# Expert layer of a small mixture-of-experts block: seven block products and one slot an expert

## What is computed

```python
h = ragged_dot(x_rep_sort, w1, group_sizes)                    # D = 1024 -> M = 3584, per expert
h = silu(h) * ragged_dot(x_rep_sort, w3, group_sizes)
out_sort = ragged_dot(h, w2, group_sizes)                      # M = 3584 -> D = 1024
out = einsum('tkd,tk->td', out_rep, topk_w)                    # two experts a token
x = x + out
```

## Time and profile before

| | us |
|---|---|
| Median of 3 runs (lowest, highest) | 8400.37 (8398.75, 8401.36) |
| The profiled execution, own time | 8408.29 |
| Its span, first to last instruction | 8406.7 |

### The profile page before, as it was taken

How to read it: one execution, slowest core, us unless ns; L and a number is a source line. 1 busy time by engine, 2 the same in 40 slices (tenths; PEclk the granted TensorE clock), 3 DMA queues, 4 the chain that set the end, 5 groups by cost and what they waited for, 6 DMA issues and landing times.

```text
span 8406.7 us, 119512 instructions
## 1 busy us (share of the span) xinstructions
PE 8220.8 (98%) x46092; PEld 7566.7 (90%) x46093; DVE 3531.5 (42%) x3602; ACT 3267.5 (39%) x3511; POOL 478.6 (6%) x580
## 2 busy tenths in 40 slices
PE   8959999999999999999999999999999999999998
PEld 5549999999999999999999999999999999999998
DVE  6755333443443334453333334453333334433343
ACT  2325333443333334453333334453333333433343
POOL 2320000000000000000000000000000000000000
PEclk8969999999999999999999999999999999999999
DMA  3335444553443434553434434554434344444343
GB/s 113 115 111 185 142 135 135 179 162 131 139 149 122 147 120 151 169 185 120 141 129 134 141 128 150 161 187 142 135 130 139 120 145 141 152 143 135 130 154 116
DMA packets 839095, 1189.77 MB, mean 142 GB/s; under 512 B 27872, under 2 KB 722400, under 8 KB 839072
## 3 DMA queue, kind: packets, MB, share of 16 engines
q1 hardware_dynamic: 812096, 1116.05, 40.5%
q0 software_dynamic: 26976, 73.42, 3.7%
HBM read 1121.90 MB, written 71.67 MB: 142 GB/s over the span
## 4 chain that ended last, share of the span: by engine, by line
PE 92%; ACT 0%; issue 0%; DVE 0%; DMA 0%; ACTq 0%; POOL 0%; POOLq 0%; DVEq 0%
PE p L1038 20%; PE p L1040 20%; PE p L1039 20%; PE acc L1063 10%; PE acc L1064 10%; PE acc L1062 10%; PE p L1093 1%; DVE lo L975 0%; ACT hi L921 0%; ACT L921 0%; DMA out_x<-y,id_s 0%; DMA xg<-x_rows,id_g 0%; DVE xlo L1001 0%; ACT xhi L946 0%; ACT y L963 0%
## 5 line engine op out<-in xcount | busy, mean ns | idle before, releaser
L1038 PE MATMUL p<-xhi,hi 128*128 128x384 f32 (+4 forms) x10752 | 3435.3, 320 | 30.6 <-DVE lo L975 19.1
L1040 PE MATMUL p<-xhi,lo 128*128 128x384 f32 (+4 forms) x10752 | 3432.7, 319 | 0.0
L1039 PE MATMUL p<-xlo,hi 128*128 128x384 f32 (+4 forms) x10752 | 3430.0, 319 | 0.0
L1038 PEld LDWEIGHTS p<-xhi,hi 128*128 128x128 f32 x10752 | 2029.1, 189 | 65.7 <-issue 41.3
L1039 PEld LDWEIGHTS p<-xlo,hi 128*128 128x128 f32 x10752 | 2030.5, 189 | 24.3
L1040 PEld LDWEIGHTS p<-xhi,lo 128*128 128x128 f32 x10752 | 2028.1, 189 | 0.0
L988 DVE TENSOR_TENSOR hid<-sil,p 128x384 f32<-128x384 f32 x672 | 372.4, 554 | 3764.0 <-PE p L1040 3764.0
L975 DVE TENSOR_TENSOR lo<-raw,hi 128x2048 fp32r<-128x2048 f32 x673 | 1543.4, 2293 | 792.8 <-ACT hi L921 792.8
L1062 PE MATMUL acc<-hi,hhi 128*128 128x512 f32 x3808 | 1497.6, 393 | 0.0
L1064 PE MATMUL acc<-hi,hlo 128*128 128x512 f32 x3808 | 1491.5, 392 | 0.0
L1063 PE MATMUL acc<-lo,hhi 128*128 128x512 f32 x3808 | 1490.6, 391 | 0.0
(11 more groups left out here) (181 smaller groups left out, 2439.4 us busy)
## 6 DMA issues: line engine op xcount, KB each, us to landing
raw<-in_L_ffn_w SPq DMA_DIRECT2D x1011, 1024.0 KB, 5.1
xin<-in_x SPq DMA_DIRECT2D x8, 2048.0 KB, 10.7
out_x<-x SPq DMA_DIRECT2D x32, 512.0 KB, 2.9
x_rows<-x SPq DMA_DIRECT2D x32, 512.0 KB, 3.7
ctxt<-in_ctx SPq DMA_DIRECT2D x4, 1024.0 KB, 9.6
table<-rec,posi POOLq DMA_INDIRECT x80
xg<-x_rows,id_g POOLq DMA_INDIRECT x75, 6.7
out_x<-y,id_s POOLq DMA_INDIRECT x72, 7.3
```

The lines of the kernel that those rows point to most:

```text
L1038: pe.matmul(bank[:, 0:n], hi13[par][:, a, k, :], xhi[:, k, 0:n], start=(k == 0), stop=False)
L1039: pe.matmul(bank[:, 0:n], hi13[par][:, a, k, :], xlo[:, k, 0:n], start=False, stop=False)
L1040: mm = pe.matmul(bank[:, 0:n], lo13[par][:, a, k, :], xhi[:, k, 0:n], start=False, stop=(k == KT - 1))
```

## The change

The attention part stays. In the expert stage the loops, the tiling and all buffers are new.

- **Slots.** A slot takes up to 1088 rows of one expert. Its rows are dealt to two halves (even and odd), and the width n of all matmuls is half the row count, rounded up to 8 and then to one of eight widths from 256 to 544. Above 512, a matmul is issued as two of n/2 columns into two PSUM banks. ScalarE and VectorE know three widths: 512, 528 and 544.
- **First product by seven block products.** A unit is one of w1, w3 with 256 hidden values. The weights (two halves of hidden values by two halves of the input, `KH` = 4 blocks each) and the rows (two halves of input by two halves of rows) are taken as 2 x 2 block matrices, and their product is formed by seven products of blocks and of sums of blocks, in place of eight. 28 units make a slot. GpSimd forms the four sums of weight blocks (`weight_sums`), ScalarE and VectorE split the seven parts (`weight_hi`, `weight_lo`), each into its one place in `wh`, `wl`, and VectorE combines the seven results (`s1`, `u2`, `v` and four outputs). The products accumulate in four pairs of PSUM banks; an accumulation goes on in a bank (`begin` False) after a partial value was read from it.
- **Through memory.** The hidden values of a pair of units (4 x 128 x n) are stored to `hd` in memory by SP, after silu and product (`store_hidden`).
- **Second product.** A second phase in the slot runs four passes, one for each half of the outputs and half of the rows. Each has 28 steps, one for each block of 128 hidden values: SP loads 128 x 512 of w2 (256 KB) and 128 x 544 of `hd` (272 KB), ScalarE and VectorE split both (`w2_hi`, `h_hi`, `w2_lo`, `h_lo`; two buffers of each), TensorE does four output blocks by three terms (`down`). Now w2 is stationary and the hidden values move, so the result stands transposed. At the end of a pass it is copied out (`turned_out`), turned back by 16 transposes (`turn_back`), scaled by VectorE (`rows_out`) and scattered with addition by GpSimd, up to five DMAs of 2 KB rows.
- **The next slot's rows** are gathered, turned, summed by GpSimd (`row_sums`) and split in the same four passes, between the steps: each pass begins with 16 transposes (`turn_rows`), and the seven splits stand in the order of ScalarE and VectorE behind fixed steps. Rows 1025 to 1088 are a "tail" with buffers of its own.
- **The next slot's first weights** (two loads of 1 MB) are issued by SP between steps 3 and 4, and 7 and 8 (counted in pairs), of the fourth pass.

The diff, cut to what the argument speaks of (constants; SP's step and its loads in the fourth pass; ScalarE's splits of the second product; VectorE's combinations; scaling; TensorE's two bodies; GpSimd's sums):

```diff
-SLOTS = (2 * T // P + E + 2 * E) // SB
-META = 32
-META_STEPS = 47
-GROUP = 32
...
+HALF = 512
+KH = KT // 2
+EP = 7
+PAIRS = MT // 2
+UNITS2 = 2 * PAIRS
+PRODUCTS = UNITS2 * EP
+STEPS = 4 * MT
+LOADS = (3 * MT // 2, MT // 2)
+SLOTS = 2 * T // (2 * HALF) + E - 1
+META = 16
+META_STEPS = 44
+WIDTHS = (256, 384, 448, 480, 496, 512, 528, 544)
+COLS = WIDTHS[-1]
+TAIL = COLS - 4 * P
+N8_MOST = COLS // 8
 RING = 3
...
+            def step(e, s, c, i2, par):
+                sp.wait_ge(s_w2lo, s * STEPS + c * MT + i2 * 2 + par + 1)
+                sp.wait_ge(s_hlo, s * STEPS + c * MT + i2 * 2 + par + 1)
+                load_w2(e, c, i2 * 2 + par, par)
+                load_h(c, i2 * 2 + par, par)
...
+                    loads(e, s, 3, 1, 4)
+                    sp.wait_ge(s_w2lo, s * STEPS + 3 * MT + 2)
+                    load13(e_next, 0, 0)
+                    loads(e, s, 3, 4, 8)
+                    sp.wait_ge(s_hlo, s * STEPS + 3 * MT + 2)
+                    load13(e_next, 1, 0)
+                    loads(e, s, 3, 8, MT // 2)
...
+            def w2_hi(s, t):
+                par, at, nth = t % 2, t // (3 * MT), (t - t // (3 * MT) * 3 * MT) // 2
+                down_free(s, t, t + 1)
+                act.wait_ge(s_raw2[at][par], s * (LOADS[at] * 16) + nth * 16 + 16)
+                copy(down_w(wh, par), raw2[at][par]).then_inc(s_w2hi, 1)
+            def h_hi(s, t, cols):
+                par, at, nth = t % 2, t // (3 * MT), (t - t // (3 * MT) * 3 * MT) // 2
+                down_free(s, t, t + 4)
+                act.wait_ge(s_rawh[at][par], s * (LOADS[at] * 16) + nth * 16 + 16)
+                copy(down_h(wh, par)[:, 0:cols], rawh[at][par][:, 0:cols]).then_inc(s_hhi, 1)
...
+                def gate(q, n):
+                    dve.wait_ge(s_sil, pr * 3 + n)
+                    V.tensor_tensor(hid[:, q, 0:cols], sil[:, q, 0:cols], hid[:, q, 0:cols], ALU.mult
...
+                product_done(s, i, a, 2)
+                dve.wait_ge(s_s1, g + 1)
+                plus(in_sbuf(u2, cols), in_sbuf(s1, cols), in_psum(b2, cols)).then_inc(s_u2, 1)
+                after(2)
...
+                plus(in_sbuf(v, cols), in_sbuf(s1, cols), in_psum(b2, cols)).then_inc(s_v, 1)
+                dve.wait_ge(s_v, g + 2)
+                plus(in_sbuf(to[:, 3], cols), in_sbuf(v, cols), in_psum(b4, cols)).then_inc(s_c22, 1)
+                after(4)
+                if a == 1:
+                    dve.wait_ge(s_c22, g + 1)
+                    gate(3, 1)
+                product_done(s, i, a, 5)
+                plus(in_sbuf(to[:, 1], cols), in_sbuf(v, cols), in_psum(b5, cols)).then_inc(s_c12, 1)
+                after(5)
+                if a == 1:
+                    dve.wait_ge(s_c12, g + 2)
+                    gate(1, 2)
...
+            def rows_out(s, c, cols):
+                nh = c // 2
+                dve.wait_ge(s_wt, s + 1)
+                if c > 0:
+                    dve.wait_ge(s_sc, s * 320 + 80 * c)
+                else:
+                    dve.wait_ge(s_hst, s * (PAIRS * 16) + PAIRS * 16 + 16)
+                for j in range(5 if cols > BANK else 4):
+                    dve.wait_ge(s_yt, s * 20 + 5 * c + j + 1 + 5)
+                    p = TAIL if j == 4 else P
+                    from_ = pair[0][0:p, 1, :] if j == 4 else pair[j][:, 0, :]
+                    V.tensor_scalar((ys + [ys_tail[c]])[j][0:p, :], from_, wt_s[0:p, j * 2 + nh:j * 2 + nh + 1], None, ALU.mult
...
+            def unit(s, u, n):
+                g = s * UNITS2 + u
+                base = s * PRODUCTS + u * EP
+                def product(e, to, begin):
+                    pe.wait_ge(s_wlo, base + e + 1)
+                    for k in range(KH):
+                        ks = slice(k * P, (k + 1) * P)
+                        for i, (w, x) in enumerate(((wh, xh), (wh, xl), (wl, xh))):
+                            for c, lo, hi in parts_of(n):
+                                mm = pe.matmul(to[:, c, 0:hi - lo], entry(w, e)[:, ks], x[:, e, k, lo:hi],
+                                               start=begin and k == 0 and i == 0, stop=k == KH - 1 and i == 2,
+                                               skip_group_check=True)
+                    mm.then_inc(s_prod, 1)
+                pe.wait_ge(s_xlo, s * (4 * EP) + 4 * EP)
+                pe.wait_ge(s_tlo, s * EP + EP)
+                pe.wait_ge(s_ys, s * 20 + 5)
+                pe.wait_ge(s_c11, g + 1)
+                product(0, b1, True)
+                pe.wait_ge(s_c21, g + 1)
+                product(1, b4, True)
+                pe.wait_ge(s_v, g + 1)
+                product(2, b2, True)
+                pe.wait_ge(s_s1, g + 1)
+                product(3, b1, False)
+                pe.wait_ge(s_u2, g + 1)
+                product(4, b2, False)
+                pe.wait_ge(s_c12, g + 1)
+                product(5, b5, True)
+                pe.wait_ge(s_c22, g + 1)
...
+                    t = s * STEPS + c * MT + i2 * 2 + par
+                    pe.wait_ge(s_w2lo, t + 3)
+                    pe.wait_ge(s_hlo, t + 3)
+                    def part_of(d, w, h, begin=False, end=False):
+                        for ch, lo, hi in parts_of(n):
+                            mm = pe.matmul(pair[d][:, ch, 0:hi - lo], down_w(w, par)[:, d * P:(d + 1) * P],
+                                           down_h(h, par)[:, lo:hi], start=begin, stop=end, skip_group_check=True)
+                        return mm
+                    if par == 0:
+                        with pe.If(i2 == 0):
+                            pe.wait_ge(s_c11, s * UNITS2 + UNITS2 + 1)
+                            pe.wait_ge(s_c12, s * UNITS2 + UNITS2 + 1)
+                            pe.wait_ge(s_c21, s * UNITS2 + UNITS2 + 1)
+                            for d in range(4):
+                                pe.wait_ge(s_ys, pass_ * 5 + (5 if d == 0 and n > BANK else d + 1))
+                                if n > BANK:
+                                    pe.wait_ge(s_quad, s * 16 + c * 4 + 16 + d + 1)
+                                part_of(d, wh, wh, begin=True)
+                        with pe.Else():
+                            for d in range(4):
+                                part_of(d, wh, wh)
+                    for d in range(4):
+                        if par == 1:
+                            part_of(d, wh, wh)
+                        part_of(d, wh, wl)
+                        mm = part_of(d, wl, wh, end=True)
...
+            def weight_sums(s, i, a, fresh=False):
+                A11, A12, A21, A22 = (raw13[a][:, kh * KH:(kh + 1) * KH, mt * P:(mt + 1) * P]
+                                      for mt in range(2) for kh in range(2))
+                before = s * PRODUCTS + i * (2 * EP) + a * EP - EP
+                done = s * (PAIRS * 8) + i * 8 + a * 4
+                pool.wait_ge(s_raw13[a], s * (PAIRS * 16) + i * 16 + 16)
+                def free(e):
+                    if not fresh:
+                        pool.wait_ge(s_wlo, before + e + 1)
+                free(1)
+                G.tensor_tensor(sums[:, 0, :, :], A11, A21, ALU.subtract).then_inc(s_sum, 1)
+                free(4)
+                G.tensor_tensor(sums[:, 1, :, :], A21, A22, ALU.add).then_inc(s_sum, 1)
+                pool.wait_ge(s_sum, done + 2)
+                free(2)
+                G.tensor_tensor(sums[:, 2, :, :], sums[:, 1, :, :], A11, ALU.subtract).then_inc(s_sum, 1)
+                pool.wait_ge(s_sum, done + 3)
+                free(5)
+                G.tensor_tensor(sums[:, 3, :, :], A12, sums[:, 2, :, :], ALU.subtract).then_inc(s_sum, 1)
```

1016 lines of the change are left out of this document (701 added, 315 removed).

## The result

The changed kernel took 8245.9 us (median of 4 runs, 8231.7 to 8262.8), the kernel before 8400.7 in the same session: a ratio of 0.9817, interval 0.9805 to 0.9829. It is faster, as forecast, but by 155 us and not by 476; the time lies 46 us above the end of the range. All times here are medians of such runs, taken without one run of e2 at 10391.7 us, which was in a slow state. The profiled execution took 8231.72 us for a span of 8230.1, which answers to the earlier trace rows.

What follows compares the result with a forecast made beforehand. TensorE, busy 98%, was taken as the bound. Start 620 + warm-up 5 + matmuls 6962 + joints 201 + queued waits 90 + clock 20 + end 32 = 7930 us of span, times 0.999 a forecast of 7924; range 7800 to 8200.

Steps and rivals of the forecast that it cites:

- New matmuls: TensorE's matmuls in both products, eight slots at columns / 2.4 per ns plus 13 ns: 6962 us against 7652 before.
- Hiding beside the first product: First product: VectorE's 9.7 us, ScalarE's under 8 and GpSimd's additions hide within a unit of 18.5 to 21.2 us.
- my bound of 4.6: First product: a GpSimd addition may take nearly 4.6 us before four fill a unit; each us beyond costs 900 us.
- the guess of 1.4: Guessed us for one GpSimd addition of 512 columns, twice VectorE's 0.69, in a range without a row.
- The loads' ring: Second product: load, landing and split take 5.1 us per two steps, fitting 5.3 to 6.05; no steady stall.
- rival 1: Second product: loads landing in 4.6 us or more set the pace, losing about 470 us; chance 0.08 for slower than 8417.
- Queued behind waits: Small loads behind 1 MB loads (40 us), gathers (32) and a slot's last scatter on GpSimd (18): 90 us, 0 to 200.
- Rival 2: GpSimd's sums bind the first product, or hold up VectorE's second-product splits, 128 us, so 8050; chance 0.12.
- Joints: TensorE's waits at ends of passes and slots, tail turns and changes between products: 201 us, in place of 139.
- The clock: TensorE stretches at 1.2 GHz after longer pauses at joints, perhaps a dozen: 20 us, 0 to 70.
- Start and end: First product begins at 620 us (605 to 640); from the last matmul to the end 32 us.
- Rival 1's partial loss: Second product: landings of 3.7 to 4.5 us, or stalls of 0.2 us a step, give 8050 to 8380; chance 0.22.

Runs made afterwards that it cites:

- e2: Changed kernel with each 1 MB load of the next slot's weights in four 256 KB pieces, one behind every second step's loads: 8202.7 us.
- e11: e9 with loads of w2 and hidden rows in passes 0 to 2 bringing only half of their columns: 8051.8 us (one run).
- e4: Changed kernel with all scatter rows out of bounds, so scatters are issued but move no data: 8144.8 us.
- e10: e9 with four widths, so four bodies of TensorE code, in place of eight; same matmuls: 8027.9 us.
- e13: Changed kernel with four widths (496, 512, 528, 544) in place of eight, nothing else changed: 8177.9 us.
- e12: e9 with all scatter rows out of bounds, so no scatter data is moved: 8026.8 us (one run).
- e1: Changed kernel with the last 1.1 MB store of hidden rows issued behind the loads of steps 2 to 5: 8223.7 us.
- e3: Changed kernel with GpSimd's four row sums of a pass on 8 of 128 columns: 8209.3 us.
- e9: e7 with the last hidden store in four pieces and the next slot's weight sums on VectorE instead of GpSimd: 8100.8 us.
- e7: Changed kernel with e1, e2 and e5 together, and a scatter's additions issued two steps apart: 8129.6 us.
- e5: Changed kernel with the four row sums of a pass in the second product made by VectorE instead of GpSimd: 8176.9 us.

## Why the prediction failed, by its own steps

- **New matmuls, 6962: measured 7046.** Slot count and widths were as read from the old widths: 496, 496, 544, 512, 528, 512, 528, 528. The prices for halves held: 528 rows took 2 x 0.123 us, 544 2 x 0.125 to 0.126. Not so those of whole banks: 0.2322 to 0.233 for 512, where I took 0.227 from the earlier trace rows, and 0.223 in the first product and 0.230 to 0.232 in the second for 496, where I had 0.220. It is 83 us. In the kernel before, a train of 512-column matmuls starts at 0.224 to 0.236 and comes to 0.2265 after ten; I read the settled end; over a whole train of 18 the mean there is 0.229, so part of the difference stood in the trace of before. In the changed kernel the irregular part doesn't end within the first product. Half the traffic (e11), no scatters (e4) and fewer bodies (e10) left the distance at 512 as it was; what makes it is open.
- **Hiding beside the first product.** Right: GpSimd's additions took 1.3 to 1.7 us, under my bound of 4.6 and near the guess of 1.4, and units ran without idle time but the first and the last.
- **The loads' ring, rival 1.** Right in the steady state: landings of 3.0 and 3.3 us against 2.75 to 3.0, and most steps at TensorE's pace. What I feared, a steady stall, did not come; what came is a stall wherever another transfer runs beside the loads.
- **Queued behind waits, 90 with ends at 0 and 200: measured 253.** The term that failed most. It had three items. The place of the 1 MB loads (40 us) was right in size: e2 gave 43. So was the last scatter's queue on GpSimd ahead of the second unit's sums (18 us): in the changed kernel TensorE's waits by "issue" lay over it, and in e13 it is the 20.1 us of waits for `part`. The gathers (32 us) were priced too high: in e12, which keeps them, passes 1 to 3 hold 16 us over steady, 8 of them the joint. The term had no scatter beside the loads of the next pass, since I counted the scatter by GpSimd's time to issue it and not by the 1.06 MB that it reads, adds and writes: 101 us by e4, 74 by e12. It had no store ahead of the loads of pass 0: 22 us by e1. And two transfers at once cost more than one and one (67 at steps 7 and 8 of pass 3, against 26 and 26).
- **Rival 2, GpSimd and VectorE hold each other up.** Priced at 128 us and given 0.12; it is true, at 41 us for the row sums (e3, 37 us in the time) and about 25 for the weight sums in pass 3 (e9). I had put a row sum beside every step's slack of 0.4 us; it bites in one step of a pass, step 3, where ScalarE's and VectorE's extra work on gathered rows has already taken the slack. The Trainium skill (SBUF — State Buffer, section Who interferes with whom) told it before any row did: a VectorE instruction with two SBUF inputs and a GpSimd instruction that reads SBUF exclude each other. The traces agree: 2.95 us for a pair that takes 1.31, and in e7 3.65 for a split of 0.71. The estimate by the Trainium skill (GPSIMD Engine Reference, section 3.1), 1.2 us for an addition of 512 elements, is under the 1.3 to 1.7 measured.
- **Joints, 201: measured 215,** of which e13 took 28, so that without the code they are 187. The mechanism was right, the price per joint a little high. What came on top of that, and the 50 us of the first units in part, is code: nothing in the sum stood for it. The row that should have warned was not among mine: the change gives TensorE eight bodies for each of two products, and I counted instructions only by their run time. The Trainium skill (Runtime: NRT & Kernel Launch, section Instruction fetch mechanics) has the rule: a taken branch whose target is not in the window of instructions at hand makes the engine wait for a fetch. The trace agrees in kind (57.7 us of "issue" with eight bodies, 0.3 with four); the size of the window no run here shows.
- **The clock, 20 with ends at 0 and 70: at most some 64.** Half clock went with the waits: 191 us in the changed kernel, 154 with four bodies, 72 in e10. So its cost falls with theirs, and it is no term of its own size.
- **Start and end.** 618.8 for 620, 35 for 32.
- **The range.** Its upper end was the forecast plus 276 us, and held the ends of two terms at once (queues at 200, clock at 70), with nothing for code and little for the second product's start. Rival 1's partial loss, 8050 to 8380 with 0.22, had the measured time in it by another cause.

e10, at 8027.9 us, beats the changed kernel by 218 us and the kernel before (8397.3 in its session) by 369, with the same matmuls. It lies in the range of the prediction, but that does not bear out the sum: e10 also does without things that the sum had counted, such as the whole 1 MB loads, and the 83 us of matmul distance are still in it.

## What to carry to other kernels

Where a loop of small loads has slack of tenths of a us, list every other transfer that can run beside it, by bytes and not by issue time, and keep two large ones from starting together. Work with two SBUF inputs moved to GpSimd is not free while VectorE has such work on the path: it can be cheaper to leave it on VectorE, which did the same row sums in less than half of the time. And waits that the profile puts down to "issue", with many packets on an instruction queue, can mean that a kernel has more bodies of code than it uses; cutting those that no input needs cost one line here and gave 68 to 73 us.

## What the runs showed of the hardware that was not expected

- With eight bodies of unrolled code for each product TensorE stood still before or early in the first product of a slot, 13 times, for up to 14.5 us: 57.7 us in a run. With four bodies it was 0.3, and the packets of q8 21 and not 74 (changed kernel, e13).
- Two transfers that start together on different queues, a 1 MB load and a scatter of 1.06 MB, cost 67 us at two steps over eight slots; with the load in four pieces or the scatter's data gone it was 26 (e2, e4).
- A VectorE subtraction with both inputs in SBUF took 0.69 us alone (e5) and 3.65 beside two of GpSimd's additions (e7), more than the 1.76 of one of those: it was held for both.
- Matmuls of 512 columns in a long train were 0.2322 to 0.233 us apart, in every variant of the kernel; the short trains before had 0.229 in the mean and 0.2265 at their end. What makes the difference is open.
- The wait that one engine has for its code can lie over another wait: with the first gone, one of 3.9 us for VectorE showed at 20.1 (changed kernel, e13).
